# The widest self-attention of a decoder kernel: one exponential in place of two, and a copy on VectorE

## The reference, cut to what matters

```
x = _layernorm(x + _L1_attn_ref(x, L1_attn_Wq, L1_attn_Wk, L1_attn_Wv, L1_attn_Wo), axis=-1)

N_HEAD = 16; N_KV_HEAD = 4; HEAD_DIM = 64
q, k = rotary(x @ Wq), rotary(x @ Wk); v = x @ Wv      # k and v repeated four times over the heads
att = jnp.einsum('bhtd,bhsd->bhts', q, k) / math.sqrt(D)
att = jnp.where(tril, att, -jnp.inf)
att = jax.nn.softmax(att, axis=-1)
y = jnp.einsum('bhts,bhsd->bhtd', att, v)
return y.transpose(0, 2, 1, 3).reshape(B, T, H * D) @ Wo
```

## Time and profile before

| | us |
|---|---|
| median of three executions (3423.49 to 3437.12) | 3428.81 |
| the profiled execution, its own time | 3442.46 |
| its span, first to last instruction | 3440.7 |
| span of the widest self-attention, 1205 to 1692 | 487 |

### The profile page before, as it was taken

The page is one execution under the profiler, slowest core; times in us unless marked ns, Lnnn a source line. Parts: engine busy times, 40 slices in busy tenths (PEclk is TensorE's granted clock), DMA queues, the critical chain, the costliest instruction groups (busy, mean ns, idle before and its releaser), DMA issues. The chain is left out here.

```text
span 3440.7 us, 43169 instructions
## 1 busy us (share of the span) xinstructions
PE 2570.2 (75%) x14826; PEld 1451.9 (42%) x14826; DVE 1818.7 (53%) x5030; ACT 1327.1 (39%) x2732; POOL 982.2 (29%) x802
## 2 busy tenths in 40 slices
PE   6888885785725688888775688796776888669786
PEld 3323334563513233333452455473443333347575
DVE  4476655465748655555324568044332877546413
ACT  4335451453411266666413200224313455458521
POOL 1045660245256466666403200001001101103100
PEclk9979997897967799999987889897698799869898
DMA  3221101700545411111003000201002322030122
GB/s 106 71 58 40 40 2 34 250 23 14 165 124 94 107 29 44 43 37 36 14 18 75 11 16 12 107 4 29 13 0 76 39 27 27 12 94 2 57 99 74
DMA packets 185954, 182.60 MB, mean 53 GB/s; under 512 B 55449, under 2 KB 152474, under 8 KB 184974
## 3 DMA queue, kind: packets, MB, share of 16 engines
q1 hardware_dynamic: 176334, 167.35, 17.3%
q0 software_dynamic: 9408, 12.56, 2.4%
HBM read 121.68 MB, written 61.59 MB: 53 GB/s over the span
## 5 line engine op out<-in xcount | busy, mean ns | idle before, releaser
L929 POOL TENSOR_TENSOR l1a_p_lo<-res,l1a_p_hi 128x1024 f16<-128x1024 f32 x192 | 311.9, 1644 | 174.6 <-ACT res L1170 174.6
L1179 ACT ACTIVATE l0a_probs<-ps 128x1024 f32<-128x1024 f32 (+1 forms) x192 | 145.5, 810 | 175.4 <-PE ps L1033 103.1
L1179 ACT ACTIVATE l3a_probs<-ps 128x1024 f32<-128x1024 f32 (+1 forms) x192 | 146.9, 809 | 144.3 <-PE ps L1033 117.2
L1169 ACT ACTIVATE l1a_p_hi<-ps 128x1024 f16<-128x1024 f32 x192 | 157.8, 822 | 110.5 <-PE ps L1033 81.5
L1030 PE MATMUL ps<-l1a_qs,l1a_ks 128*128 128x512 f16 (+3 forms) x768 | 166.3, 331 | 32.1 <-ACT res L1170 32.1
L1201 DVE CUSTOM_DVE_ANT_0 l1a_masked<-ps,l1a_wide_mask 128x128 bf16<-128x128 f32 (+3 forms) x256 | 118.0, 490 | 102.9 <-PE ps L999 100.6
L999 PE MATMUL ps<-l1a_ks,l1a_qs 128*128 128x512 f16 (+3 forms) x384 | 121.3, 344 | 63.2 <-DVE l1a_nmax L1204 33.0
L954 POOL TENSOR_TENSOR l0a_both<-l0a_probs 128x768 f32<-128x768 f32 (+2 forms) x96 | 154.7, 1633 | 46.6 <-PE ps L1071 46.4
L2828 PE MATMUL ps<-x_m,x_x 128*128 128x462 f16 (+1 forms) x672 | 138.9, 355 | 31.3 <-PEq L111 30.7
L1170 ACT ACTIVATE res<-ps 128x1024 f32<-128x1024 f32 x192 | 158.1, 823 | 0.0
L1033 PE MATMUL ps<-mask_t,ident_b 128*128 128x128 bf16 x768 | 157.9, 225 | 0.0
(11 more groups left out here) (710 smaller groups left out, 6283.3 us busy)
## 6 DMA issues: line engine op xcount, KB each, us to landing
f_w<-in_L_ffn_w_dram SPq DMA_DIRECT2D x16, 1024.0 KB, 6.3
f_slots<-x0a_zeros SPq DMA_DIRECT2D x32, 256.0 KB
f_xe<-f_slots SPq DMA_DIRECT2D x32, 256.0 KB, 3.0
f_ys<-f_y SPq DMA_DIRECT2D x32, 256.0 KB
l1a_qs<-l_q_h SPq DMA_DIRECT2D x64, 128.0 KB
d_wall<-in_L_ffn_W_dram SPq DMA_DIRECT2D x3, 2112.0 KB
l0a_qs<-l_q_h SPq DMA_DIRECT2D x32, 128.0 KB
l0a_ks<-l_k_h SPq DMA_DIRECT2D x16, 256.0 KB
```

The source lines that it names most:

```text
L929: pool.tensor_tensor(ph_lo[:, n % SLOTS, :, 0:w], probs[:, n % FULL, :, 0:w], ph_hi[:, n % SLOTS, :, 0:w], ALU.subtract).then_inc(s_["low_ ...
L1169: act.activation(ph_hi[:, n % SLOTS, :, 0:w], SB[n % 2][:, :, 0:w], ACT.Exp)
L1179: act.activation(probs[0:KR, n % SLOTS, 2 * pr:2 * pr + 2, 0:w], SB[x % 2][:, :, 0:w], ACT.Exp).then_inc(s_["exps"], 1)
```

## The change: what it does

ScalarE computes one exponential for a unit, the one in float32. VectorE then copies the float32 tile into the f16 tile (`upper(n)`), as its last work for unit n, after the items beside the unit and ahead of an inversion. GpSimd's subtraction waits for this copy instead of the exponentials. The wait for a free `ph_hi` slot moves from ScalarE to VectorE. The names of the counts change (`low_pool` and `low_dve` become `lows`), and the branch for a subtraction on VectorE goes.

```
-                        if not by_dve(n):
-                            pool.wait_ge(s_["exps"], n + 1)
-                            pool.tensor_tensor(ph_lo[...], probs[...], ph_hi[...], ALU.subtract).then_inc(s_["low_pool"], 1)
+                        pool.wait_ge(s_["uppers"], n + 1)
+                        pool.tensor_tensor(ph_lo[...], probs[...], ph_hi[...], ALU.subtract).then_inc(s_["lows"], 1)
...
     def values(n):
-                        pe.wait_ge(s_["low_pool"], pool_lows)
+                        pe.wait_ge(s_["lows"], n + 1)
...
     block.scalar, unit n:
-                        if n >= SLOTS:
-                            act.wait_ge(s_["values"], n - SLOTS + 1)
                         if n >= FULL:
-                            (wait for low_pool or low_dve of unit n - FULL)
+                            act.wait_ge(s_["lows"], n - FULL + 1)
                         act.wait_ge(s_["b_done"], n + 1)
-                        act.activation(ph_hi[:, n % SLOTS, :, 0:w], SB[n % 2][:, :, 0:w], ACT.Exp)
                         act.activation(probs[:, n % FULL, :, 0:w], SB[n % 2][:, :, 0:w], ACT.Exp).then_inc(s_["exps"], 1)
...
+                def upper(n):
+                    w = QC - units[n][1].off
+                    if n >= SLOTS:
+                        dve.wait_ge(s_["values"], n - SLOTS + 1)
+                    dve.wait_ge(s_["exps"], n + 1)
+                    dve.tensor_copy(ph_hi[:, n % SLOTS, :, 0:w], probs[:, n % FULL, :, 0:w]).then_inc(s_["uppers"], 1)
+
                 for n in range(U):
                     for part in beside[n]:
                         for a in part:
                             item(a)
-                    if split and by_dve(n):
-                        (wait for exps, subtract on VectorE)
+                    if split:
+                        upper(n)
                     for s in invert_after[n]:
                         invert(s)
```

More of the change, by code:

```diff
@@ L775, in packed_attention @@
     FULL = 3
[L777 to L783, removed]
     LOADS = LEAD // 2 + 2
@@ L829, in packed_attention @@
         spread = ph.sb("spread", [P, P], F16)
-        ph.sems_of("cleared zeroed k_filled q_filled a_done maxed merged split b_done exps values evac recips inverted loading gated c_ld joined v_upper v_lower low_pool low_dve mask_ready added totaled")
+        ph.sems_of("cleared zeroed k_filled q_filled a_done maxed merged split b_done exps values evac recips inverted loading gated c_ld joined v_upper v_lower uppers lows mask_ready added totaled")
         ld = [ph.sem(f"ld{i}") for i in range(LOADS)]
@@ L926, in _ @@
                         w = QC - u.off
-                        if not by_dve(n):
-                            pool.wait_ge(s_["exps"], n + 1)
-                            pool.tensor_tensor(ph_lo[:, n % SLOTS, :, 0:w], probs[:, n % FULL, :, 0:w], ph_hi[:, n % SLOTS, :, 0:w], ALU.subtract).then_inc(s_["low_pool"], 1)
+                        pool.wait_ge(s_["uppers"], n + 1)
+                        pool.tensor_tensor(ph_lo[:, n % SLOTS, :, 0:w], probs[:, n % FULL, :, 0:w], ph_hi[:, n % SLOTS, :, 0:w], ALU.subtract).then_inc(s_["lows"], 1)
                     return
@@ L1245, in _ @@
                             item(a)
-                    if split and by_dve(n):
-                        w = QC - units[n][1].off
-                        dve.wait_ge(s_["exps"], n + 1)
-                        dve.tensor_tensor(ph_lo[:, n % SLOTS, :, 0:w], probs[:, n % FULL, :, 0:w], ph_hi[:, n % SLOTS, :, 0:w], ALU.subtract).then_inc(s_["low_dve"], 1)
+                    if split:
+                        upper(n)
                     for s in invert_after[n]:
```

3 lines of the change are left out of this document (removed).

## The result

Median of 18 executions each: 3451.84 us after (3440.49 to 3459.56), 3437.23 us before (3423.49 to 3454.64), ratio 1.0041 with a 95% interval from 1.0029 to 1.0053. The change costs 14.6 us by the medians where +31 was forecast. The profiled execution spans 3453.3 us, 12.6 more than before. The direction was right and the time lies in the range, 3443 to 3480 us, but at 0.4% the outcome is "within 0.5%" (the interval just reaches past it), to which the prediction gave 20 in 100. That the time lies inside the range is in part luck: the forecast was laid on a median of three executions, 3428.81 us, and the kernel before came out at 3437.23 this time. On the old median the measured difference would give 3443.4 us, the very edge of the range.

The account below looks back on a forecast made before the run. The prediction took the attention stage to be bound by waits among four engines. Its new period, 19.73 + 6.62 + 1.1 + 5.36 = 32.8 us against 30.86, times 16 gave +31 us: 3428.81 + 31 = 3460 us, range 3412 to 3497 (forecast's own 3443 to 3480).

Parts of the forecast that it names:

- The stage is a loop of waits, with ScalarE's second exponential off the path: Attention stage, 487 us: no engine fills it, TensorE busiest at 398.6; the removed exponential was counted as no gain.
- Price of a copy, 0.681 us from a row with 16 partitions: VectorE's full-width copy, priced from a measured cast; 6.62 us a period over all widths, 106 us in all.
- The upper end of 1.226: VectorE's copy at its dearest, as long as a two-tensor subtraction: up to 80 us more in all, 3 in 100.
- Copy and subtraction alternate: VectorE's copy and GpSimd's subtraction never run beside each other, so the copies' 6.62 us a period add to 19.73.
- The first rival (overlap): Copies run beside GpSimd's subtractions, about half of 5.3 us hides; period 30.1 us, -12 us, 3417 us; 14 in 100.
- Inversion and maxima in line at a step's start: The first unit's copy stands behind VectorE's inversion and maxima: 2 x 0.79 + 1.88 + 1.90 = 5.36 us a period.
- 12 x 0.09 = 1.1: Hand-overs around GpSimd's subtractions, 0.07 us after its release and 0.02 us to VectorE's: 1.1 us a period.
- third rival: Worse than the sum: slower TensorE clock, 3495 us, or the inversion's DMA wait on top, 45 us; 12 in 100.
- ScalarE's relief decides: Second rival: the path after every evacuation loses one exponential, 0.90 us x 32 = 29 us, to 3400 us; 10 in 100.
- TensorE starves and its clock falls: TensorE's pauses grow, clock 0.91 instead of 0.99, matmuls take 35 us more, 3495 us; 12 in 100.
- One sign of the forecast: TensorE's maxima matmuls in the attention stage were to wait longer than 42.8 us for VectorE.

Follow-up runs that it names:

- e1: The change without its copy, f16 tile filled once with a constant, subtraction waiting for the exponential alone; ratio to the kernel before 1.0068, period 33.05 us.
- e3: The change with each unit's copy ahead of its maxima instead of behind them, nothing left out; ratio to the kernel before 1.0037, period 32.1 us.
- e9: The change with the copy written as a maximum reduction over an axis of length 1, same place and waits; ratio to the kernel before 1.0023, period 31.5 us.
- e2: The change with its copy cut to 8 columns per head, order and waits unchanged; ratio to the kernel before 0.9946, period 29.5 us.
- e12: The kernel before with SyncE's nine loads of queries and keys issued one step later; ratio to the kernel before 0.9927, period 29.08 us.
- e6: The change with the inversion moved behind the second unit of the step after; ratio to the kernel before 1.0217, period 35.8 us.
- e5: The kernel before with the inversion moved behind the second unit of the step after; ratio to the kernel before 0.9963, period 31.0 us (29.1 or 35).

## Why the prediction was right or wrong

- **The stage is a loop of waits, with ScalarE's second exponential off the path:** right. Taken away alone it even costs time (e1).
- **Price of a copy, 0.681 us from a row with 16 partitions:** right; 0.68 unheld on 128 partitions. The straight line was drawn through the two rows, so the second row could not confirm it, as the text has it; the unheld copies of e3 do, with 0.55, 0.42 and 0.28 us. The upper end of 1.226 had no part.
- **Copy and subtraction alternate:** right; e9 shows that it is the plain copy's form that is held, and e2 what its length costs. The first rival (overlap) fell.
- **Inversion and maxima in line at a step's start:** right in size. The two holes of the period from 1246.27 are 3.23 and 3.52 us, 6.75 together; the forecast's are 5.36 + 2 x (0.681 + 0.09) = 6.90. Part of that is luck. Behind the long step the inversion runs mostly beside the last subtraction, which the forecast had ruled out, and a wait for TensorE fills its place:

```profile
1264.11 0.17 DVE L1213 SCALAR_TENSOR_TENSOR l1a_r_parts<-l1a_r_col,l1a_r_parts 128x8 f16<-128x8 f32 x1
1264.70 0.29 DVE L1182 CUSTOM_DVE_ANT_0 l1a_masked<-ps,l1a_wide_mask 128x128 bf16<-128x128 f32 x1 [0.43 <-PE ps L990]
```

- **The step that failed** is the sum of copies and hand-overs in the runs, "12 x 0.09 = 1.1" on top of 6.62. A held copy adds 0.63, 0.49, 0.44 (or 0.36) and 0.23 us by width, hand-over included, not 0.77, 0.64, 0.51 and 0.38. Over the ten copies that aren't first in a step that is 4 x 0.63 + (0.49 + 0.44 + 0.23) + (0.49 + 0.36 + 0.23) = 4.76 us instead of 6.16. The period came out at 31.4 and not 32.8, and these 1.4 us are the difference of the periods: 16 x 1.4 = 22 us, where the periods give +8 for the forecast's +31. That a copy's fixed start and the hand-over pass while it is held would explain it; no run isolates this.
- **What the forecast did not see** is why the copies cost so little on balance. The copies add 4.8 us to GpSimd's runs and lengthen the period by 0.5. The kernel before carried a loss of its own, SyncE's late DMA and the hold behind it, worth 1.8 us a period (e12), in the very place where the change makes GpSimd stand still: VectorE's DMA wait fell by 25 us, 1.6 a period, and the hold of the inversion's first instruction went. That the one paid for the other is read from the traces and not shown by a run; e12's edit on the change would be the test. The text had the DMA wait only as something that might come on top (third rival).
- **ScalarE's relief decides:** wrong by e1. **TensorE starves and its clock falls:** not in the change, whose stage ran at 1.00; it is what happened in e1 and e6 (0.94 in both). One sign of the forecast failed with it: TensorE's weight loads for the maxima wait 32.0 us for the reductions of L1185, where they waited 42.8 for the same reductions and were to wait longer.
- The periods give +8 us, the stage +11.3, the runs +14.6; the 3 us between stage and runs is not explained, nor is it above what the profiled executions differ by.

## What to carry to other kernels

Before an engine's work is shortened, look at what starts earlier for it and whose turn that takes: here GpSimd ran into VectorE's inversion. A copy on VectorE from SBUF to SBUF next to a busy GpSimd is to be costed as a turn in a queue, here subtraction plus 0.63 us at full width, and read from the pitch and not from the copy's length. A wait for a tiny DMA at a step's start should be followed back to the issuing queue first: moving nine loads by one step gave more than any other edit here.

## What was not expected of the hardware

- Instructions of 8 elements a partition are held by GpSimd as long as those of 1024: 2.01 and 2.04 us instead of 0.17, twice in a row (e5). A reciprocal of the same size never was: it takes 0.20 us in the stage of every kernel, also in e6, where 27 of 32 lie wholly inside subtractions.
- A held copy costs less than its own length: 0.63 us behind a subtraction, 0.68 alone; with 256 elements 0.23 us, alone 0.27 to 0.29.
- After a pause of 4.21 us TensorE's first matmul of 512 columns took 0.39 us and one 1.35 us later 0.63, with the granted clock down from 1.00 to 0.50 (e1): the slow stretch came after the pause and not at once.
